# Two edits in the first layer of a two-layer graph network: row numbers copied by another engine, and narrower matmuls for two of three products

## The reference, cut to what matters

```python
f_s, f_v = _fctp_scalar_attr(xs, xv, Wl1_0, Wl1_1, a)     # node features, projected
h = jax.nn.gelu(edge_scalar_attr @ Wfc1 / np.sqrt(8.0))
h = jax.nn.gelu(h @ Wfc2 / np.sqrt(64.0))
w = h @ Wfc3 / np.sqrt(64.0)                              # 192 weights per edge
gs = f_s[edge_src]                                        # gather of node rows
gv = f_v[edge_src]
mid0 = w0 * gs * y0[:, None]
mid1 = w3 * jnp.einsum('euc,ec->eu', gv, y1) * INV_SQRT3
mid2 = (w1 * gs)[:, :, None] * y1[:, None, :]
mid3 = w2[:, :, None] * gv * y0[:, None, None]
seg = lambda x: jax.ops.segment_sum(x, edge_dst, num_segments=N) * inv
```

## Time and profile before

| | |
|---|---|
| median of 3 runs | 2860.58 us (2855.46 to 2861.92) |
| the profiled execution | 2861.52 us |
| its span, first to last instruction | 2859.5 us |
| mean granted clock of PE | 0.935 of full speed |
| first layer's gathers, first and last start | 89.6 and 1136.3 us |
| node stage | 1148 to some 1302 us |
| second layer | from there to some 2790 us |
| last stage | the rest |

### The profile page before, as it was taken

The page is one execution under the profiler, slowest core; times in us unless marked ns, Lnnn a source line. Parts: engine busy times, 40 slices in busy tenths (PEclk is TensorE's granted clock), DMA queues, the critical chain, the costliest instruction groups (busy, mean ns, idle before and its releaser), DMA issues. The chain is left out here.

```text
span 2859.5 us, 80951 instructions
## 1 busy us (share of the span) xinstructions
PE 2562.2 (90%) x24172; PEld 2200.9 (77%) x24172; DVE 1627.0 (57%) x4318; ACT 882.3 (31%) x1939; POOL 2082.1 (73%) x1874
## 2 busy tenths in 40 slices
PE   4798888888888888897999999999999999999970
PEld 2577767776776676886999999999999999999960
DVE  5455555455555555434666666666666666666646
ACT  1111111111111111223444444444444444444430
POOL 3577777777777776244888888888888888888881
PEclk9999999999999989558999999999999999999985
DMA  4433333333333333236888888888888888887865
GB/s 127 120 107 96 101 96 101 99 98 100 100 100 95 99 100 80 79 153 138 143 144 141 144 142 143 145 141 143 144 143 145 141 143 143 143 144 142 143 99 166
DMA packets 388992, 355.56 MB, mean 124 GB/s; under 512 B 60993, under 2 KB 340929, under 8 KB 388417
## 3 DMA queue, kind: packets, MB, share of 16 engines
q0 software_dynamic: 150528, 141.40, 33.1%
q1 hardware_dynamic: 228256, 204.77, 25.2%
q10 hardware_dynamic: 10176, 9.03, 1.1%
HBM read 244.75 MB, written 135.90 MB: 133 GB/s over the span
## 5 line engine op out<-in xcount | busy, mean ns | idle before, releaser
L684 POOL DMA_INDIRECT tab<-summed,sidx x784 | 1217.7, 1553 | 272.8 <-issue 212.2
L637 POOL DMA_INDIRECT gat<-f,gidx x784 | 762.5, 973 | 272.7 <-issue 229.1
L1145 DVE TENSOR_TENSOR prod<-ps_w,xg 128x768 f32<-128x768 f32 x392 | 375.4, 958 | 281.5 <-issue 161.5
L935 PE MATMUL ps_o<-ro_v,prod 128*128 128x96 f32 x3136 | 478.2, 275 | 0.0
L935 PEld LDWEIGHTS ps_o<-ro_v,prod 128*128 128x128 f32 x3136 | 413.2, 192 | 0.0
L1014 DVE TENSOR_TENSOR ta<-ps_w,gat 128x512 f32<-128x512 f32 x196 | 135.5, 691 | 446.6 <-DMA gat<-f,gidx 421.3
L925 PE MATMUL ps_w<-hid,wf 64*128 64x128 f32 x4704 | 368.7, 289 | 1.2 <-DVE prod L1145 1.2
L771 ACT ACTIVATE xg<-ps_x 128x768 f32<-128x768 f32 x392 | 296.3, 808 | 199.4 <-PE ps_x L957 194.7
L799 PEld LDWEIGHTS ps_g<-sel,ta 128*128 128x128 f32 x1568 | 203.3, 203 | 193.0 <-DVE acc_c L1026 162.5
L925 PEld LDWEIGHTS ps_w<-hid,wf 64*128 64x128 f32 x4704 | 293.5, 187 | 69.4 <-issue 44.6
L799 PE MATMUL ps_g<-sel,ta 128*128 128x96 f32 x1568 | 237.0, 298 | 120.2 <-DVE acc_c L1026 119.5
(11 more groups left out here) (182 smaller groups left out, 3274.8 us busy)
## 6 DMA issues: line engine op xcount, KB each, us to landing
src_bc<-in_src_rows SPq DMA_DIRECT2D x196, 256.0 KB
tabw<-feat SPq DMA_DIRECT2D x784, 36.0 KB
ea<-in_ea SPq DMA_DIRECT2D x196, 128.0 KB
feat<-fst SPq DMA_DIRECT2D x25, 576.0 KB, 2.9
gat<-f,gidx POOLq DMA_INDIRECT x784
hot_dst<-in_dst_rows SPq DMA_DIRECT2D x98, 128.0 KB
hot_dir<-sh_rows SPq DMA_DIRECT2D x98, 128.0 KB
dst_bc<-hot_dst SPq DMA_DIRECT2D x196, 64.0 KB
```

The costliest lines, as they stand in the source:

```text
L637: pool.indirect_dma_start(out=gat[:, r % 4, k, :], out_offset=None, in_=t["f0"], in_offset=bass.IndirectOffsetOnAxis(ap=gidx[:, r // 4, at ...
L684: pool.indirect_dma_start(out=t["tabs"][into[k]], out_offset=bass.IndirectOffsetOnAxis(ap=sidx[:, r, k:k + 1], axis=0), in_=summed[:, r, k ...
L935: last = pe.matmul(ps_o[:, k, 96 + 64 * c:192 + 64 * c], prod[:, ur % 2, k, 1 + c, :], ro_v[:, c, :], start=True, stop=True)
L1145: dve.tensor_tensor(prod[:, r % 2, :, :, :].rearrange("p k c e -> p k (c e)"), ps_w4[:, :, 0:3 * P], xg[:, r // 2, r % 2 * 2:r % 2 * 2 + 2 ...
```

## The change

It has two parts, and a longer written-out loop.

1. POOL no longer copies row numbers. ACT does, with an activation Copy, into four slots instead of two: those of the first four groups before its first GELU, and from then on, at every fourth group u, those of groups u+4 to u+7, behind the two GELUs of u and behind a wait for the products of u-9 and all before. POOL waits for that copy. POOL's and ACT's loops are written out for 16 groups instead of 8 and 2.
2. The window sums of `tb` take only the first 24 columns of `sel`, and those of `tc` only the last 72, which are the ones that are added.

```diff
-            gidx = sb(c2, "gidx", [P, 2, 4 * G], I32)
+            gidx = sb(c2, "gidx", [P, 4, 4 * G], I32)
...
                 def gather(u, j, r):
                     if r % 4 == 0:
-
-                        since(pool, prod_done, u - 4)
-                        pool.tensor_copy(gidx[:, r // 4, :], src_i[:, bass.ds(u * G, 4 * G)]).then_inc(gidx_done, 1)
-                        since(pool, gidx_done, j * 2 + r // 4 + 1)
+                        since(pool, gidx_done, j * 4 + r // 4 + 1)
                     since(pool, prod_done, u - 3)
...
-                steps(pool, NGRP, gather, 8, 8)
+                steps(pool, NGRP, gather, 16, 16)
...
-                    act.activation(h1[:, r, :], ps_h1[:, :], ACT.Gelu_apprx_tanh,
+                    act.activation(h1[:, r % 2, :], ps_h1[:, :], ACT.Gelu_apprx_tanh,
                                    scale=8.0 ** -0.5).then_inc(g1_done, 1)
                     act.wait_ge(h2_ready, u + 1)
                     since(act, w_ready, u - 1)
-                    act.activation(h2[:, r, :], ps_h2[:, :], ACT.Gelu_apprx_tanh,
+                    act.activation(h2[:, r % 2, :], ps_h2[:, :], ACT.Gelu_apprx_tanh,
                                    scale=1.0 / 8.0).then_inc(g2_done, 1)
-                steps(act, NGRP, gelus, 4, 2)
+                    if r % 4 == 0 and runs(u + 4, NGRP):
+                        since(act, prod_done, u - 8)
+                        act.activation(gidx[:, (r // 4 + 1) % 4, :], src_i[:, bass.ds(u * G + 4 * G, 4 * G)],
+                                       ACT.Copy).then_inc(gidx_done, 1)
+                act.activation(gidx[:, 0, :], src_i[:, 0:4 * G], ACT.Copy).then_inc(gidx_done, 1)
+                steps(act, NGRP, gelus, 16, 16)
...
-                for n, (lhs, hi) in enumerate(((ta, P), (tb, 96), (tc, 96))):
+                for n, (lhs, hi, lo, up) in enumerate(((ta, P, 0, 4), (tb, 96, 0, 1), (tc, 96, 1, 4))):
                     for k in range(G):
-                        last = pe.matmul(ps_g[r][0:hi, n * 4 * WIN:(n + 1) * 4 * WIN],
+                        last = pe.matmul(ps_g[r][0:hi, (n * 4 + lo) * WIN:(n * 4 + up) * WIN],
                                          lhs[:, r, k, :, :].rearrange("p a b -> p (a b)"),
-                                         sel[:, r, k, :, :].rearrange("p a b -> p (a b)"),
+                                         sel[:, r, k, lo:up, :].rearrange("p a b -> p (a b)"),
                                          start=k == 0, stop=k == G - 1)
```

## The result

| | before | changed |
|---|---|---|
| median of 4 runs (the forecast stood on the first 3 of before) | 2861.25 us (2855.46 to 2862.82) | 2824.52 us (2819.86 to 2828.20) |
| ratio to before, 95% interval | | 0.9873 (0.9862 to 0.9885) |
| profiled execution, span | 2861.52, 2859.5 us | 2825.36, 2823.5 us |
| forecast | | 2827 us, range 2815 to 2858 |

The page of the changed kernel, part 2: POOL is as busy as before, and PE's clock now falls often in the first layer.

The account below looks back on a forecast made before the run. POOL's issue rate of gathers was taken to bound the first layer. Gains of 38.8 and 0.6 us less 4.3 for the later start gave 35.1; less 2 at the layer's end, 33 us: 2860.6 to 2827 us, range 2815 to 2858.

Parts of the forecast that it names:

- What bounds the kernel: First layer: POOL's issue rate of gathers is the bound, 5.35 us per group, and stays it at 5.15.
- POOL's copies: Start of each four-group turn on POOL: 0.81 us saved, 48 times, 38.8 us in all, all on the path.
- Rival 2: Heads of POOL's turns: most of the gap is the wait's and stays, 2854 us; 6% together with the clock taking most gain.
- ACT's copy: 49 small activations on ACT, 11 us, never making POOL late except the first, which starts the layer 4.3 us later.
- The longer loop: POOL's and ACT's loop bodies written out for 16 groups: costed at nothing, with 2.0 us gaps possibly 7 us either way.
- The narrow matmuls: PE's window sums: `tb` and `tc` stay at 85 ns per matmul, set by weights, and the time changes by nothing.
- The clock: PE's granted clock in the first layer: 0.80 to 0.94 expected; PE decides once the half-clock share exceeds 0.32.
- 0.6 us back for this stretch: Near 121 us: POOL waited 0.90 us for products where 0.30 is usual; starting later it doesn't, giving 0.6 us back.
- a sign that I had named: POOL in the first layer: its wait for DVE's products under 10 us would show the forecast right.
- the layer's end: PE may be behind at half clock with two or three groups open: 0 to 12 us lost, 2 taken.
- Rival 3: First layer: the 2.0 us gaps go and nothing is lost at the end, 2818 us; 10%.
- Rival 1: PE's clock falls more often with less streaming, making it slower: 2938 us at half-clock share 0.5, 3437 at 1; 15%.

Follow-up runs that it names:

- copy2x: Kernel before with POOL copying row numbers at every second group instead of every fourth, 98 copies instead of 49: 2896.08 us against 2855.57, ratio 1.0137.
- loop16: Kernel before with only POOL's loop written out for 16 groups instead of 8, copies staying on POOL: 2854.81 us against 2855.57, ratio 0.9997.
- thin_ta: Changed kernel with sums of `ta` and `tc` narrowed to 24 columns in three of each group's four tiles: 3417.73 us against 2855.57, ratio 1.1967 to before.
- early_wide_again: Changed kernel with ACT's first copy ahead of its wait for weights and all window sums 96 columns wide: 2815.37 us against 2853.13, ratio 0.9864 to before.
- p1_again: Changed kernel with all window sums 96 columns wide as before, so ACT's copies alone: 2820.57 us against 2853.13, ratio 0.9871 to before.

## Why the prediction was right

**What bounds the kernel: right.** POOL's issue rate. With the copies gone the gathers take 39.5 us less, with twice the copies 44.0 us more (copy2x beside loop16), and the spans follow: 36.0 less, the 3.9 of the late start being lost again, and 44.4 more.

**POOL's copies: right, and too small.** Forecast 38.8 us. With them went the four gaps of 2.0 us, 6.8 us more, which I had thought might be the loop's and left at nothing; loop16, copy2x and thin_ta show that they need a wait of POOL at fixed places, and in the kernel before the copies were the only such wait. The wait that stays on POOL costs nothing: each turn now begins after 0.30 us. Rival 2 falls with that.

**ACT's copy: right.** 0.207 us each, forecast 0.22, and never late after the first. The first gather is 3.9 us later, forecast 4.3, and that it moves the whole layer is shown by the traces of early_wide_again and p1_again.

**The longer loop: right at nothing** (0.9997).

**The narrow matmuls: right on their time.** `tb` and `tc` now, at full clock, in the timeline of PE:

```profile
599.99 1.13 PE L801 MATMUL ps_g<-sel,ta 128*128 128x96 f32 x8
600.96 0.78 PE L801 MATMUL ps_g<-sel,tb 128*96 128x24 f32 x8
601.58 0.88 PE L801 MATMUL ps_g<-sel,tc 128*96 128x72 f32 x8
602.30 0.64 PE L820 MATMUL ps_h<-h,w 128*128 128x256 f32 x2
```

The sixteen of `tb` and `tc` take 1.34 us, 84 ns each, as before (1.36 us), though they move a quarter and three quarters of the columns. The weight loads set the step. The Trainium skill (TensorE: Matmul & The Clock Gate, section "LDWEIGHTS (loading the stationary operand)") gives columns of weights / 1.2 ns, an estimated 80 ns for 96 columns; the trace's 84 at full clock is near it. At half clock the formula fails: eight of `tb` take 1.28 us, 160 ns each. The estimated 12.5 ns that the Trainium skill's formula for an isolated matmul (same page, section "Back-to-back issue gap") gives for 24 columns was not seen.

**The clock: right in kind, and not free.** It went from 0.94 to 0.90, so x, the share of time at half clock, rose from 0.12 to 0.20 or a little more (the row misses the start, see below), still under the 0.32 at which PE becomes the bound. The timeline of PE shows a long stretch at half clock in which PE doesn't rest once:

```profile
549.87 2.02 PE L801 MATMUL ps_g<-sel,ta 128*128 128x96 f32 x8
551.68 1.37 PE L801 MATMUL ps_g<-sel,tb 128*96 128x24 f32 x8
552.87 1.53 PE L801 MATMUL ps_g<-sel,tc 128*96 128x72 f32 x8
554.20 1.15 PE L820 MATMUL ps_h<-h,w 128*128 128x256 f32 x2
555.28 1.66 PE L827 MATMUL ps_w<-w,h 64*128 64x192 f32 x8
556.87 1.22 PE L815 MATMUL ps_h<-ea,w 16*128 16x256 f32 x2
558.02 2.02 PE L801 MATMUL ps_g<-sel,ta 128*128 128x96 f32 x8
```

POOL, up to three groups ahead, didn't notice. It did at the start of the layer. PE stays at half clock there until about 136 us, where the earlier trace rows show full clock by 118, and POOL waits 1.44 and 3.88 us, 4.7 more than usual. The first two rows are of the changed kernel, with the last slow `ta` and the first fast one; the third is its stretch, with the granted clock again given as 1.00 where the steps are slow; the fourth is p1_again, which starts as late but has wide sums, is at full clock at 118.80 and never makes POOL wait:

```profile
129.54 2.02 PE L801 MATMUL ps_g<-sel,ta 128*128 128x96 f32 x8
137.04 1.13 PE L801 MATMUL ps_g<-sel,ta 128*128 128x96 f32 x8
118.00:137.00 19.00, 19.00 (x84) 14.28 (x83) 6.63 (x19) 2.02 (x6) 12.34 (x13) 1.00 0.30 82
118.80 1.13 PE L801 MATMUL ps_g<-sel,ta 128*128 128x96 f32 x8
```

So the 4.7 us come with the narrow sums, whose effect on the time I had put at nothing. Forecast was 0.6 us back for this stretch; it is the one term with the wrong sign, and with it a sign that I had named was missed: POOL's waits for DVE's products are 14.8 us and not under 10. At the layer's end I took 2 us, and measured 0.4 less than nothing.

**The sum.** Forecast -38.8 + 4.3 - 0.6 + 2 = -33.1. Afterwards: copies -38.8 (the forecast's own working, which copy2x supports; no row measures it by itself), gaps -6.8, later start +3.9, waits for products +4.7 less the 0.6 that went, POOL's gathers themselves +2.3 (764.8 us instead of 762.5), end -0.4, which gives -35.7; the spans differ by 36.0. The +2.3 is no effect of the change that can be told: the same 784 gathers took 756.2 us in loop16. That 2827 came within 3 us of 2824.52 is in part luck. The gaps (6.8 too little gain) were set off by the waits (4.7 too much), and the end (2.4 too much loss) by the gathers.

**Rival 3** had both of its conditions come true, the gaps gone and nothing lost at the end. That the time was not its 2818 us is due to the waits at the layer's start and the slower gathers.

**Rival 1** didn't happen here, and thin_ta shows that it is real and near: a further cut of the same kind costs 562 us. Where PE is the bound for another reason, this edit already costs 1%. What stays open is why PE pauses in that setting, and what narrowing `tb` and `tc` alone does to the time where POOL is the bound: the 4.7 us of waits are from traces of two sessions, and the times don't resolve them.

## What to carry to other kernels

Find the engine whose idle time has no releaser before trusting busy shares: PE at 89% was not the bound, POOL at 74% was, and a 0.2 us copy on it cost 0.8 us each time because of the wait for its own result. Don't cut moving columns from matmuls whose weight loads set the pace: nothing is won, and TensorE's clock may pay for it. When an edit is worth nothing by the sum, ask whether a bundle needs it: the copies without the narrow sums have the same time, within what was measured, and a higher clock (0.96 instead of 0.90).

## What the runs showed that I had not expected

Gaps of 2.0 us in POOL's gathers, with no releaser, at every 26th group and only where POOL had just waited: four with 49 copies, seven with 98, seven in thin_ta without a copy, none in the changed kernel. Less streaming made this kernel 20% slower, since PE stayed at 1.2 GHz for 1550 us while busy all the time. The granted clock read 1.00 for stretches at half clock at the layer's start and through all of thin_ta's; step times tell. And the kernel before took some 365 us more on three of the five chips of the experiments, and every variant traced there was bound by PE and not by POOL.
